# A transformer block with routed experts on one core: tile 0 projected in plain float32, rows loaded ahead of weights, late sums taken a step later

## What is computed

```python
x = L0_attn_x                                   # (4, 1024, 512), float32
x = _layernorm(x + _L0_attn_ref(x, Wq, Wkv, q_scale, k_scale, Wg, bg, Wo))
x = _layernorm(x + _L0_ffn_ref(x, gate_w, w1, w2, w3, ws1, ws2, ws3))

# attention: 8 heads of 128, a window of this and the previous 128 rows
q = l2norm(x @ Wq.T) * q_scale ; k = l2norm(x @ Wk.T) * k_scale ; v = x @ Wv.T
o = softmax(mask(8 * q @ k.T)) @ v * sigmoid(x @ Wg.T + bg)
return o @ Wo.T
# experts: 8 experts, the best 2 of each row by softmax, and a shared one for all rows
h = silu(x @ w1[e].T) * (x @ w3[e].T) ; y += weight * (h @ w2[e].T)
z = silu(x @ ws1.T) * (x @ ws3.T) @ ws2.T
```

## Time and profile before

| what | value |
|---|---|
| three runs | 1603.62, 1608.31, 1607.5 us (median 1607.5) |
| the profiled execution | 1604.93 us |
| span of it, first to last instruction | 1602.8 us |
| TensorE (PE) busy | 1566.6 us, 98% |
| DVE, ACT, POOL busy | 59%, 45%, 42% |
| stage A | until about 1082 us |
| stage B | until the end |

### The profile page before, as it was taken

The page is one execution under the profiler, slowest core; times in us unless marked ns, Lnnn a source line. Parts: engine busy times, 40 slices in busy tenths (PEclk is TensorE's granted clock), DMA queues, the critical chain, the costliest instruction groups (busy, mean ns, idle before and its releaser), DMA issues.

```text
span 1602.8 us, 31930 instructions
## 1 busy us (share of the span) xinstructions
PE 1566.6 (98%) x9650; PEld 1387.0 (87%) x9651; DVE 938.6 (59%) x2565; ACT 718.2 (45%) x1624; POOL 679.5 (42%) x636
## 2 busy tenths in 40 slices
PE   7999999999999999999999999999899999999898
PEld 6899999989999999989999999987778888888786
DVE  5555555655556555665565655657655555555376
ACT  4434333443334433443334333446455555655354
POOL 3323333243333432334324333253355555555375
PEclk9999999999999999999999999999999999999999
DMA  8111111111111111111112111139688888888993
GB/s 288 57 60 62 38 34 34 45 54 33 33 33 60 39 33 33 47 52 33 33 33 65 33 33 33 52 114 219 165 214 223 221 215 226 215 222 216 291 387 124
DMA packets 100960, 176.27 MB, mean 110 GB/s; under 512 B 11742, under 2 KB 28638, under 8 KB 100336
## 3 DMA queue, kind: packets, MB, share of 16 engines
q1 hardware_dynamic: 79360, 134.76, 24.9%
q0 software_dynamic: 20064, 40.86, 13.8%
q10 hardware_dynamic: 1488, 0.04, 0.1%
HBM read 128.04 MB, written 57.02 MB: 115 GB/s over the span
## 4 chain that ended last, share of the span: by engine, by line
PE 89%; DMA 6%; DVE 2%; issue 2%; POOL 1%; ACT 1%; SPq 0%; POOLq 0%; DVEq 0%; ACTq 0%
PE bank L1236 33%; PE bank L1159 14%; PE bank L1334 12%; PE bank L1311 7%; PE bank L1187 7%; PE bank L1285 6%; PE bank L1269 3%; PE bank L1298 3%; PE bank L1135 2%; DMA bx<-x_d 2%; DMA w_raw<-in_w2T 1%; PE bank L1170 1%; DMA passing<-in_wqkvT 1%; DMA gb<-eo_d 1%; DMA bx<-x_d,idxc 1%
## 5 line engine op out<-in xcount | busy, mean ns | idle before, releaser
L1236 PE MATMUL bank<-wh,xh 128*128 128x512 f32 (+2 forms) x896 | 339.1, 378 | 1.6 <-DVE wl L1450 1.5
L1236 PE MATMUL bank<-wl,xh 128*128 128x512 f32 (+2 forms) x896 | 327.6, 366 | 0.0
L1236 PE MATMUL bank<-wh,xl 128*128 128x512 f32 (+2 forms) x896 | 326.9, 365 | 0.0
L723 POOL TENSOR_TENSOR rnorm<-ssmax,nhalf 128x4 f32<-128x4 f32 x128 | 131.8, 1030 | 389.2 <-DVE ssmax L1488 383.9
L1236 PEld LDWEIGHTS bank<-wh,xh 128*128 128x128 f32 x896 | 170.2, 190 | 28.4 <-DVE wl L1450 2.1
L1236 PEld LDWEIGHTS bank<-wh,xl 128*128 128x128 f32 x896 | 170.0, 190 | 28.2
L1236 PEld LDWEIGHTS bank<-wl,xh 128*128 128x128 f32 x896 | 170.5, 190 | 22.3
L908 ACT ACTIVATE sq<-bank 128x512 f32<-128x512 f32 x128 | 75.7, 591 | 169.6 <-PE bank L1236 166.6
L1496 DVE TENSOR_TENSOR qkn<-bank,rnorm 128x512 f32<-128x512 f32 x128 | 88.4, 690 | 107.6 <-POOL rnorm L723 107.6
L1334 PE MATMUL bank<-woh,oh 128*128 128x256 f32 (+1 forms) x512 | 147.8, 289 | 1.0 <-DVE xr L1558 1.0
L1483 DVE TENSOR_REDUCE ssum<-sq 128x4 f32<-128x512 f32 x128 | 87.7, 685 | 103.7 <-ACT sq L908 95.9
(11 more groups left out here) (225 smaller groups left out, 3869.2 us busy)
## 6 DMA issues: line engine op xcount, KB each, us to landing
w_raw<-in_w2T SPq DMA_DIRECT2D x71, 512.0 KB
eo_d<-zero_d SPq DMA_DIRECT2D x36, 256.0 KB, 3.0
xt<-in_xT SPq DMA_DIRECT2D x33, 256.0 KB, 3.2
xr<-in_x SPq DMA_DIRECT2D x32, 256.0 KB, 2.7
x_d<-xr SPq DMA_DIRECT2D x32, 256.0 KB, 2.1
eo_d<-xr SPq DMA_DIRECT2D x32, 256.0 KB, 2.3
w_f<-in_w13T SPq DMA_DIRECT2D x8, 1024.0 KB, 11.7
ga<-eo_d SPq DMA_DIRECT2D x16, 512.0 KB, 6.5
```

Of the source, the lines that this page charges most:

```text
L723: pool.tensor_tensor(rnorm[:, :], ssmax[:, :], nhalf[:, :], ALU.pow).then_inc(rn_s, 1)
L1236: mm = pe.matmul(b[:, 0:n], a[:, par, c, :], wt[:, c, cols], start=(c == 0 and k == 0), stop=(c == DC - 1 and k == 2))
```

## The change

Tile 0 is projected by `first_block`: plain float32 products of the landed rows `xt` with the landed weights `stage`, one block when it has landed, with no wait on a split. The split still runs, for step 1 on, and step 1 waits for it. `gate_of_wo(0)` moves behind v2. `wo_n` is loaded behind all six weight blocks. What overwrites `stage` or `xt` now also waits for the products of tile 0 (`proj`).

```diff
@@ SP, start
             for n in range(6):
                 sp.dma_start(stage[n], wqkvT[:, c0:c0 + GRP]...).then_inc(w_in[n], 16)
-                if n == 3:
-                    sp.dma_start(wo_n[:, :, :], ...).then_inc(wo_n_in, 16)
+            sp.dma_start(wo_n[:, :, :], ...).then_inc(wo_n_in, 16)
...
                 if not middle and s == 0:
                     sp.wait_ge(w_lo, 6)
+                    sp.wait_ge(proj, 7)
                     for n in range(2):
                         sp.dma_start(wo_raw[...
@@ POOL, before the clearing of kTh and kTl (and SP, before xt of tile 2: proj, 7)
             pool.wait_ge(w_lo, 2)
+            pool.wait_ge(proj, 2)
@@ PE
+            def first_block(name, b):
+                i = W_LOADS.index(name) if name != "v2" else 5
+                n = GRP // 2 if name in ("v1", "v2") else GRP
+                c0 = GRP // 2 if name == "v2" else 0
+                pe.wait_ge(xt_in[0], 16)
+                pe.wait_ge(w_in[i], 16)
+                for c in range(DC):
+                    mm = pe.matmul(b[:, 0:n], xt[:, 0, c, :], stage[i][:, c, c0:c0 + n], ...)
+                if name == "v2":
+                    pe.wait_ge(gate_centred, 1)
+                    for k in range(2):
+                        for c in range(DC):
+                            mm = pe.matmul(b[:, n + k * H:n + (k + 1) * H], xt[:, 0, c, :], wgs[:, k, c, :], ...)
+                mm.then_inc(proj, 1)
...
                 project(s, "k1", par, first)
-                if first:
-                    gate_of_wo(0)
...
                 project(s, "v2", par, first, s_out=out_on)
+                if first:
+                    gate_of_wo(0)
@@ SP, start of stage B
+            load(3, 3)
             sp.dma_start(sh2_raw[:, :, :], ...)
-            load(3, 3)
             store_rows(NT - 2, 0)
             weights(1)
             weights(2)
             weights(3)
-            store_rows(NT - 1, 1)
             sp.wait_ge(wo_s, 2 * NT)
             load(4, 4)
+            for q in (5, 6, 7):
+                sp.wait_ge(*place_free(q, q))
+                load(q, q)
+            store_rows(NT - 1, 1)
+            for e in range(4, E):
+                weights(e)
...
-                for k in ((5, 6) if q0 == 3 else (q0 + 3,)):
-                    if kind(k) == "sh" and k < FIRST + 4:
+                for k in ((q0 + 5,) if q0 < S1 - 5 else (q0 + 3,)):
+                    if kind(k) == "sh" and not S1 - 5 <= q0 < S1 and k < FIRST + 4:
                         sp.wait_ge(*place_free(k, k))
                         load(k, k)
-                if 3 <= q0 < E - 1:
-                    weights(q0 + 1)
@@ the end
-        zs = sbuf(s3, "zs", [P, 2, D])
+        zs = sbuf(s3, "zs", [P, 4, D])
-            if q0 >= FIRST + 2:
-                return bank_sum, q0 - FIRST - 1
+            if q0 >= FIRST + 4:
+                return bank_sum, q0 - FIRST - 3
-        ORDER = [0, 7, 1, 8, 2, 9, 3, 10, 4, 11, 5, 12, 6, 13, 14, 15]
-        AT = [4, 5, 6, 7, 8, 9, 10, 11, 12, 13, 14, 15, 16, 17, 19, 20]
-        FROM_BANK = EARLY + 1
+        ORDER = [0, 1, 8, 2, 9, 3, 10, 4, 11, 5, 12, 6, 13, 7, 14, 15]
+        AT = list(range(5, 21))
+        FROM_BANK = EARLY + 2
@@ DVE, a step of stage B
-                if FIRST + 2 <= q0 - 1 < NQ - 2:
+                if FIRST + 4 <= q0 - 1 < NQ - 2:
                     bank_total(q0 - 1)
```

More of the change, by code:

```diff
@@ L480, in _ @@
                 sp.dma_start(stage[n], wqkvT[:, c0:c0 + GRP].rearrange("(c p) n -> p c n", p=P)).then_inc(w_in[n], 16)
-                if n == 3:
-                    sp.dma_start(wo_n[:, :, :], wo.rearrange("(c p) k -> p c k", p=P)).then_inc(wo_n_in, 16)
+            sp.dma_start(wo_n[:, :, :], wo.rearrange("(c p) k -> p c k", p=P)).then_inc(wo_n_in, 16)
             def weights(e):
@@ L507, in step @@
                         settled(sp)
+                    if not middle and s == 1:
+                        sp.wait_ge(proj, 7)
                     sp.dma_start(xt[:, 1 - par, :, :],
@@ L601, in step @@
                     load_second(q + 1, q0 + 1)
-                for k in ((5, 6) if q0 == 3 else (q0 + 3,)):
-                    if kind(k) == "sh" and k < FIRST + 4:
+                for k in ((q0 + 5,) if q0 < S1 - 5 else (q0 + 3,)):
+                    if kind(k) == "sh" and not S1 - 5 <= q0 < S1 and k < FIRST + 4:
                         sp.wait_ge(*place_free(k, k))
                         load(k, k)
-                if 3 <= q0 < E - 1:
-                    weights(q0 + 1)
                 if q0 == FIRST:
                     sp.wait_ge(h_s, FIRST)
-                    for i in range(3):
+                    for i in range(2):
                         load_four(i)
@@ L615, in step @@
                         load_pair(n)
-                        if n == 3:
-                            load_four(3)
+                        if n in (2, 4):
+                            load_four(n // 2 + 1)
                 if pair_at(q0) is not None:
@@ L818, in add_pair @@
                 pool.wait_ge(g_in[b], 32 * (n // NB) + 32)
-                if ORDER[n] == EARLY:
+                if EARLY <= ORDER[n] < FROM_BANK:
+                    k = ORDER[n] - EARLY
                     pool.tensor_tensor(ga[:, b, :, :], ga[:, b, :, :], gb[:, b, :, :], ALU.add).then_inc(y_s, 1)
-                    pool.wait_ge(y_s, 1)
-                    pool.wait_ge(res_s2, S1 + 2)
-                    pool.tensor_tensor(ga[:, b, :, :], ga[:, b, :, :], zs[:, :, :], ALU.add).then_inc(gab_s, 1)
+                    pool.wait_ge(y_s, k + 1)
+                    pool.wait_ge(res_s2, S1 + 2 * k + 2)
+                    pool.tensor_tensor(ga[:, b, :, :], ga[:, b, :, :], zs[:, 2 * k:2 * k + 2, :], ALU.add).then_inc(gab_s, 1)
                     return
@@ L889, in _ @@
             weight_high(1)
-            weight_high(2)
             def weight_hi(e, chunks=slice(0, DC)):
@@ L974, in step @@
                 if first:
-                    weight_high(3)
+                    weight_high(2)
                     act.wait_ge(gate_centred, 1)
@@ L979, in step @@
                     squares(0, 1, 1)
+                    weight_high(3)
                     squares(0, 2, 2)
@@ L1117, in step @@
                                    scale=slot_w[:, bass.ds(row(q - 1, q0 - 1), 1)]).then_inc(wres_s, 1)
-                if kind(q0 - 1) == "sh" and q0 - 1 < FIRST + 2:
+                if kind(q0 - 1) == "sh" and q0 - 1 < FIRST + 4:
                     take_shared(q - 1, q0 - 1)
@@ L1201, in count_choices @@
                 mm.then_inc(counts, 1)
+            def first_block(name, b):
[5 more added lines that the diff above has]
+                for c in range(DC):
+                    mm = pe.matmul(b[:, 0:n], xt[:, 0, c, :], stage[i][:, c, c0:c0 + n], start=(c == 0),
+                                   stop=(c == DC - 1))
+                if name == "v2":
+                    pe.wait_ge(gate_centred, 1)
+                    for k in range(2):
+                        for c in range(DC):
+                            mm = pe.matmul(b[:, n + k * H:n + (k + 1) * H], xt[:, 0, c, :], wgs[:, k, c, :],
+                                           start=(c == 0), stop=(c == DC - 1))
+                mm.then_inc(proj, 1)
             def project(s, name, par, first, s_out=False, group=None):
@@ L1206, in project @@
                 n = QKV_WIDTH.get(name, GRP)
+                if first:
+                    first_block(name, b)
+                    return
+                if isinstance(s, int) and s == 1:
+                    pe.wait_ge(w_lo, W_LOADS.index(name) + 1 if name != "v2" else 6)
                 if name == "q0":
@@ L1228, in project @@
                         pe.wait_ge(res_s, 2 * s - 2)
-                    if first:
+                    if isinstance(s, int) and s == 1:
                         pe.wait_ge(wg_split, 2)
-                if first and name != "v2":
-                    pe.wait_ge(w_lo, W_LOADS.index(name) + 1)
                 cols = slice(QKV_COLS[name], QKV_COLS[name] + n)
@@ L1457, in _ @@
             weight_low(1)
-            weight_low(2)
             dve.wait_ge(small_in, 48)
@@ L1569, in first_tile @@
                 sums(0, 0, True)
+                weight_low(2)
+                scale(0, 0, False)
+                sums(0, 1)
+                gate_low()
                 weight_low(3)
-                gate_low()
-                sums(0, 1)
-                scale(0, 0, False)
+                scale(0, 1, False)
                 sums(0, 2)
-                scale(0, 1, False)
                 weight_low(4)
-                weight_low(5)
                 scale(0, 2, False)
                 sums(0, 3)
+                weight_low(5)
                 scale(0, 3, False)
```

## The result

The change makes the kernel slower, by a little. Twelve runs of each: before 1605.07 us (1602.91 to 1608.31), after 1609.95 us (1605.46 to 1613.47), a ratio of 1.0025 with a 95% interval of 1.0015 to 1.0036, or 4.0 us. The profiled execution after took 1611.27 us with a span of 1609.3, so its span is 6.5 us longer than the 1602.8 of before. Forecast were 5.9 us less. The first table follows TensorE through both spans. Each row is the start of the transposes of a tile in stage B (line 1135 before, 1142 after), and how much later the changed kernel stands there.

The account below looks back on a forecast made before the run. TensorE, busy 98% of the span, was taken to bound the kernel, with its idle stretches and lower clock. Terms +4.2, -2.5 and -7.6 gave -5.9 us, from a median of 1607.5 to 1601; 8-in-10 range 1594 to 1608.

Parts of the forecast that it names:

- part 1: Head: tile 0 in plain float32 removes waits for split blocks but adds TensorE work; 4.2 us later.
- part 2: Stage B: rows of tiles 4 to 7 loaded ahead of weights, tile 8's behind four weights; 2.5 us gained.
- part 3: End: late sums a step later, removing the wait for `gTl` and the lower clock after it; 7.6 us gained.
- a start before 39: Head: tile 1 starting before 39 would show the forecast wrong; it expected a start at 41 to 42.
- tile 4's 3.6 us go for certain: Stage B: tile 4's late rows, 1.89 us, and the lower clock after them, 1.7 us, were to vanish.
- so this wait is mostly inside the other one: Stage B: TensorE's wait of 0 to 9 us for tile 8's rows falls mostly within its wait for the slots.
- its other case: Stage B: `slot_t` lands where it did; a 7 us wait and 1.7 at the lower clock, together nothing won.
- rival 2: Stage B: tile 8's rows land at 1124 or later, TensorE waits 9 us; part 2 loses 7 or more, 1614; chance 0.10.
- a landing near 1114: Stage B: tile 8's rows, never getting less than half the engines, land then; part 2 wins some 5 us.
- The pairs keep their absolute times [...], so transfers do not pile up: End: the pairs' times stay, first statistics at 1519, so transfers add no delay to the 7.6 us gain.
- The rival on this part: End: DVE waits for the third pair, 4 to 5 us of TensorE idle return; sum near -1, 1606; chance 0.15.
- on engines with room: End: two added ACT copies of 0.6 and a POOL sum of 2.4 us fit on engines with room.

Follow-up runs that it names:

- e1: Kernel before with only tile 0 in plain float32, `wo_n` behind the weights and the gate product behind v2; 1608.63 us, ratio 1.0028.
- e2: Kernel before with only rows 4 to 7 loaded ahead, weights 4 to 7 in one go and rows 8 to 11 behind them; 1607.22 us, ratio 1.0016.
- e3: Kernel before with only the late sums a step later, four places `zs` and the four loads of `xs` moved; 1600.97 us, ratio 0.9984.
- e13: Kernel before with part 1, DVE's sixth-block split ahead of its norm step, first half of `wo_raw` waiting for one block less; 1606.42 us, ratio 1.0013.
- e4: Kernel before with part 2, but rows of tiles 8 to 11 and weights of experts 4 to 7 issued in turn; 1605.34 us, ratio 1.0001.
- e8: Kernel before with rows issued as in e4, but weights of experts 5, 6 and 7 at steps 6, 7 and 8; 1604.30 us, ratio 0.9990.

## Why the prediction was wrong

It said -5.9 us and came out as +4.0, and the median of 1609.95 lies outside the range of 1594 to 1608. Its base, 1607.5 from three runs, was 2.4 us above the median of twelve; that is not what failed. By its own steps, in us:

| step | forecast | alone, by the ratio | alone, by the medians |
|---|---|---|---|
| part 1 | +4.2 | +4.5 (e1) | +4.0 |
| part 2 | -2.5 | +2.6 (e2) | +2.6 |
| part 3 | -7.6 | -2.6 (e3) | -3.7 |
| sum | -5.9 | +4.5, and +4.0 for the whole | +2.9 |

- **Part 1: the size came out right in part by luck.** A plain product costs 0.86 (forecast 0.93), and tile 1 starts at 38.15 and not 41.5; a start before 39 was one of the prediction's own signs of being wrong. By that the part was to be cheaper. It was not, because `wo_raw` did hold ACT and `scores`. The text had the splits ended "by 33 us under plain products"; they end at 35.16, behind three steps in which POOL's power took 3 us. `wo_raw` was issued at 35.20 (forecast 37.1), `scores` came at 50.3 (forecast 51.7), and e13 points to the split as the cause. In the traces the head loses 2.0 to 4.1 us, and a part of the 4.5 of the ratio lies elsewhere, so the agreement with 4.2 is not all the forecast's doing.
- **Part 2: two steps failed.** The first is "tile 4's 3.6 us go for certain". They went, and 1.6 came back a tile later as the wait for `gg`. The 1.7 in them was the lower clock behind the old wait, which the nine other kernels with a wait at that place don't have. So it was a cost of one execution, and against those nine the early rows win 0.3 us. The second is "so this wait is mostly inside the other one". The landing of tile 8's rows was put between 1114 and 1124, and the price of it inside the wait for the slots. They landed between 1126.2 and 1128.2 in the changed kernel and at 1123.3 in e2. The wait for them, 7.5 and 5.3 us, took the place of all the waits for rows that the earlier trace rows had (5.5 together) and left none for the slots, and it came with the lower clock (0.50 over 4 us in both). What was to pay for it, `slot_t` some 3 us earlier, did not come either. It landed within 2 us of where it did (1130.6 to 1133.9 in after, e2, e4 and e8), as the forecast had as its other case, so that not even e4, which keeps all rows in time, wins. The late rows are rival 2's mechanism, at well under half of its price of 7.
- The rule of the Trainium skill ("DMA: Bandwidth & Descriptors", section on queues, rings and completion order), by which an engine alternates between its queues packet by packet, gave a landing near 1114 as the prediction used it. The measurement is 1123.3 in e2 and past 1126.2 in the changed kernel. The traces agree with the rule itself: from 1120 to 1124, where both queues had work, SP's and POOL's moved 270 and 274 packets before, and 116 and 115 after. What failed is what the prediction made of it, at least half of the engines for SP. With equal numbers of packets SP's took 41% of the engines' time before and 40% after, and POOL's 68% and 62%; both together moved 257 GB/s before and 108 after. So equal turns were not equal time, and they did not fix a rate.
- **Part 3: what was removed was sized right (8.2 against 7.6); what came next was not seen.** The step that failed is "The pairs keep their absolute times [...], so transfers do not pile up". It looked at DVE and POOL, and not at ACT's wait for a place of `oo`. The trace of before had it, twice:

```profile
1535.39 1.52 ACT L1092 ACTIVATE oo<-ga,nm,rs 128x512 f32<-128x512 f32 x2 [1.70 <-DMA out<-oo]
...
1539.22 1.52 ACT L1092 ACTIVATE oo<-ga,nm,rs 128x512 f32<-128x512 f32 x2 [0.68 <-DMA out<-oo]
```

  They were short while TensorE itself stood 8 us late there. Take these 8 us away and ACT asks for the place that much earlier, while the transfers, which began when the last scatter had landed, keep their time. So the first of the two waits becomes 4.54 us in e3 and 4.69 in the changed kernel. The change also put 1 MB more (a load of `xs`) ahead of the first stores. The rival on this part had POOL's third pair as the next wait; that wait did not come (DVE waits 0.59 us before its first sum from a bank, and for TensorE).
- The 1.0 us behind the last tile is the second POOL sum of pair 7 in the fourteenth place. The text had put this POOL work "on engines with room", read from its busy share of the span and not from that place, where ACT waits 2.3 us for POOL's `nm`.

## What to carry to other kernels

When a wait is removed, list every engine that waited less because of it, and look in the trace for waits that are small today on a buffer with two places: they can grow by as much as is won (here 1.70 us grew to 4.54 when 8.2 were won). Price a wait from more than one execution: the lower clock that comes with it in one trace may be missing in the next. Rows that are wanted soon go ahead of weights that are wanted late in a queue, and rows behind the weights wait for all of them. If a head is bound by an in-order list on DVE or ACT, faster products only move the wait; look first at the last item in that list that a transfer waits for.
